# The order of GpSimd's work around the seam between attention and experts, in a spiking-attention and mixture-of-experts kernel

## The reference

```
Q, K, V = spike(layer_norm(xn @ W.T + b) * gain + beta - 1)        # values 0 or 1, 16 heads of 16
out     = einsum((16 - hamming(Q, K) + log_position_bias) * scale, V)
s       = spike(layer_norm(spike(out - 0.5) @ Wo.T + bo) * go + betao - 1)

xr      = rms_norm(xn);  ids = nearest of 8 centroids, for each row
h       = xr @ up_w[ids]  (256 -> 1024);  a, g = halves of h
y       = (a * silu(g)) @ down_w[ids]     (512 -> 256)
result  = x + s * silu(y + xn)
```

## Time and profile before

| | us |
|---|---|
| median of 3 runs | 425.05 |
| lowest and highest | 421.77, 425.44 |
| profiled execution, its own time | 424.03 |
| its span, first to last instruction | 422.2 |
| mean granted TensorE clock in it | 0.962 of full |

### The profile page before, as it was taken

The page is one execution under the profiler, slowest core; times in us unless marked ns, Lnnn a source line. Parts: engine busy times, 40 slices in busy tenths (PEclk is TensorE's granted clock), DMA queues, the critical chain, the costliest instruction groups (busy, mean ns, idle before and its releaser), DMA issues.

```text
span 422.2 us, 10208 instructions
## 1 busy us (share of the span) xinstructions
PE 380.5 (90%) x2652; PEld 319.7 (76%) x2662; DVE 326.6 (77%) x821; ACT 237.5 (56%) x614; POOL 246.7 (58%) x338
## 2 busy tenths in 40 slices
PE   5596999999997697999499999999999999999992
PEld 5475878778875586888378888888888888888881
DVE  5965888888867989886557767778777787878883
ACT  1555877878875053463445555555555565555551
POOL 1444777778865044456827656665666666666542
PEclk9888999999998898999879999999999999999997
DMA  6448456866630020231651222222222223221100
GB/s 198 167 148 276 147 154 178 259 225 186 184 117 2 0 77 26 76 104 49 183 191 46 84 80 63 69 78 91 87 70 75 84 81 103 92 89 57 37 15 0
DMA packets 31649, 44.86 MB, mean 106 GB/s; under 512 B 4041, under 2 KB 25714, under 8 KB 31492
## 3 DMA queue, kind: packets, MB, share of 16 engines
q1 hardware_dynamic: 25040, 29.38, 22.6%
q0 software_dynamic: 6240, 14.71, 11.7%
q10 hardware_dynamic: 340, 0.42, 0.3%
HBM read 36.28 MB, written 15.61 MB: 123 GB/s over the span
## 4 chain that ended last, share of the span: by engine, by line
PE 60%; DMA 10%; DVE 10%; POOL 7%; issue 7%; ACT 3%; POOLq 1%; SPq 1%; DVEq 0%; ACTq 0%
PE bank L558 22%; PE bank L576 12%; DMA xs<-in_x 6%; PE bank L400 6%; PE bank L446 4%; PE bank L540 4%; DMA row_a<-rows_a,slot_id 3%; PE bank L478 3%; PE bank L529 2%; POOL inv_std L1142 2%; PE bank L450 2%; POOL sq L1167 2%; PE bank L458 1%; DVE up_lo L1039 1%; POOL rs L1161 1%
## 5 line engine op out<-in xcount | busy, mean ns | idle before, releaser
L1079 DVE TENSOR_TENSOR d_lo<-down_sb,d_hi 128x1024 fp32r<-128x1024 f32 x39 | 47.8, 1226 | 33.2 <-ACT d_hi L739 33.2
L1204 POOL DMA_INDIRECT row_a<-rows_a,slot_id x39 | 40.1, 1029 | 46.8 <-DVE e_o L1093 44.9
L739 ACT ACTIVATE d_hi<-down_sb 128x1024 fp32r x39 | 41.3, 1060 | 45.3 <-PE bank L576 33.2
L1248 POOL DMA_INDIRECT out_x<-e_o,slot_id x39 | 44.6, 1142 | 20.6 <-issue 14.4
L558 PE MATMUL bank<-up_hi,e_xh 128*128 x156 | 52.5, 418 | 0.0
L1210 POOL DMA_INDIRECT row_s<-rows_s,slot_id x39 | 41.0, 1050 | 15.7 <-issue 11.6
L558 PE MATMUL bank<-up_lo,e_xh 128*128 x156 | 48.7, 393 | 0.0
L558 PE MATMUL bank<-up_hi,e_xl 128*128 x156 | 48.4, 391 | 0.0
L400 PE MATMUL bank<-w_hi,x_hi 128*128 128x264 f32 (+1 forms) x128 | 42.3, 412 | 0.8 <-DVE dots L888 0.8
L664 ACT ACTIVATE junk<-bank 128x256 bf16<-128x256 f32 x96 | 36.0, 379 | 9.1 <-PE bank L404 8.2
L687 ACT ACTIVATE junk<-bank 128x256 bf16<-128x256 f32 x32 | 12.0, 379 | 50.1 <-PE bank L480 50.1
(11 more groups left out here) (210 smaller groups left out, 1036.6 us busy)
## 6 DMA issues: line engine op xcount, KB each, us to landing
up_raw<-in_up_w SPq DMA_DIRECT2D x16, 512.0 KB, 5.1
rows_a<-xn SPq DMA_DIRECT2D x32, 128.5 KB, 2.5
xs<-in_x SPq DMA_DIRECT2D x8, 512.0 KB, 3.4
rows_a<-in_x SPq DMA_DIRECT2D x8, 512.0 KB, 5.5
down_sb<-in_down_w SPq DMA_DIRECT2D x8, 512.0 KB, 4.5
rows_s<-s_out SPq DMA_DIRECT2D x8, 256.0 KB, 2.4
blk_tab<-in_blocks SPq DMA_DIRECT2D x1, 1024.0 KB, 5.6
row_a<-rows_a,slot_id POOLq DMA_INDIRECT x39, 3.4
```

What stands on the lines that cost most here:

```text
L739: act.activation(d_hi[:, :, :], down_sb[:, bass.ds(e, 1), :, :].rearrange("p a c n -> p (a c) n"), ACT.Copy).then_inc(d_high, 1)
L1079: V.tensor_tensor(d_lo[:, :, :], down_sb[:, bass.ds(e, 1), :, :].rearrange("p a c n -> p (a c) n"), d_hi[:, :, :].bitcast(F32), ALU.subtra ...
L1204: G.indirect_dma_start(row_a[s % 4][:, :], None, rows_a, bass.IndirectOffsetOnAxis(ap=slot_id[:, s:s + 1], axis=0), bounds_check=N - 1, oo ...
L1248: G.indirect_dma_start(out, bass.IndirectOffsetOnAxis(ap=slot_id[:, s:s + 1], axis=0), e_o[s % 4][:, :], None, bounds_check=N - 1, oob_is_ ...
```

## The change

On POOL, in the attention loop. `norms_out` of the chunk comes first in every chunk. The clearing of the row buffers, with its waits, moves from chunk 5, ahead of the norms, to chunk 4, behind the norms and ahead of the low part of expert 6. The first four `gather_a` stood directly behind the clearing; now tiles 0 and 1 are gathered in chunk 5 behind the norms, and tiles 2 and 3 in chunk 6 behind the norms. The low part of expert 7 moves from between the norms of chunks 6 and 7 to behind the norms of chunk 7. In chunks 0 to 3 the order is the same. No other engine's code changes.

```diff
--- before.py
+++ after.py
@@ -1220,7 +1220,8 @@
             for e in range(2):
                 low_part_up(e)
             for c in range(NCH):
-                if c == 5:
+                norms_out(c % 2, c // 2)
+                if c == 4:
                     pool.wait_ge(slots_made, 1)
                     for k in range(4):
                         G.memset(row_a[k][:, :], 0.0)
@@ -1230,13 +1231,12 @@
                         pool.wait_ge(row_put[k], 16 * NT // 4)
                     pool.wait_ge(x_copied, 16 * NT // 4)
                     pool.wait_ge(rows_clear, 1)
-                    for k in range(4):
-                        gather_a(k)
-                norms_out(c % 2, c // 2)
                 if c < NCH - 3:
                     low_part_up(c + 2)
-                if c == NCH - 2:
-                    low_part_up(E - 1)
+                if c in (5, 6):
+                    for k in range(2):
+                        gather_a(2 * (c - 5) + k)
+            low_part_up(E - 1)
             for k in range(2):
                 pool.wait_ge(s_put[k], 16 * NCH // 2)
             for k in range(4):
```

## The result

| | us |
|---|---|
| changed kernel, median of 20 runs | 421.62 (417.88 to 423.35) |
| kernel before, median of 20 runs beside them | 425.46 (421.30 to 428.19) |
| ratio | 0.990, 95% interval 0.9878 to 0.9923 |
| changed kernel once more on another chip (below) | ratio 0.9904, interval 0.9872 to 0.9936 |
| profiled execution, its span | 419.71, 417.9 |

The change saves 3.84 us by the medians, and 3.3 to 5.2 by the interval. The prediction was 419.8 in 417.0 to 423.0, so the direction and the range held; the saving is 1.4 us smaller than the 5.2 between the forecast and the median that it started from.

The account below looks back on a forecast made before the run. POOL's order, clearing and gathers ahead of norms 5, was taken to hold PE at the seam. Profiled 424.03 - 4.8 = 419.2 and median 425.05 - 4.8 = 420.3 gave a forecast of 419.8 us, range 417.0 to 423.0.

Parts of the forecast that it names:

- The bound and the cause: Between attention and experts, PE idles 5.71 us for a_sp of chunk 7; POOL's order costs PE some 6 us, once.
- ACT next, then the loads: At the experts' start: ACT's unmoved e_xh holds PE until 208.1, then down-weight loads landing at 212.4 hold tile 0's silu.
- The size: At e_h of expert tile 0: 213.2 instead of 218.02, 4.8 us less, with unchanged work from there.
- faster by over 1%: Whole kernel: time falls by more than 4.25 us; chance 0.57, against 0.38 within 1% and 0.05 slower.
- I take 0: Chunk 4: the moved clearing slows DVE's low parts by 0 more; up to 1.2 us was left for the upper end.
- The low part of expert 7 "nothing": POOL: moving this 2.47 us piece behind norms 7, to about 211.3, costs nothing, as it ends before s_out has landed.
- The first gather: POOL, chunk 5: starts at 199.7, lands at 203.3, or 205.2 if slowed; lateness up to 1.5 us hides.
- a first gather after 205.6: Sign at the seam: the forecast would be wrong if the first gather landed later than 205.6.
- Rival 2: Experts' start: loads land at 213.7 and PE's clock falls; 1.9 us less, 422.7, or 421.2 with only one; chance 0.27.
- rival 1: Experts' start: loads land by 211.3 and DVE's order decides; e_h at 212.1, 5.9 us less, 418.5; chance 0.14.
- Rival 4: Experts' stage: reuse of four row buffers costs 1.4 us per two tiles; 434 at ten such rounds; chance 0.04.

Follow-up runs that it names:

- the last experiment: Changed kernel plus ACT's load wait behind the first silu and expert 7's ACT and DVE parts moved later, gathers two by two; ratio to the kernel before 1.0000.
- norms-first kernel: Kernel before with only the norms of chunk 5 moved ahead of the clearing and all four gathers; ratio to the kernel before 1.0011.

## Why the prediction was right, and where it was off

- **The bound and the cause** held: PE's wait was POOL's order, by way of s_out of chunk 5 and a_sp of chunk 7. The wait is gone with the order, and early loads alone move nothing.
- **ACT next, then the loads** held, to a tenth: e_xh at 208.1 was forecast, 208.36 - 0.67 (the anchor's difference) = 207.69 came. The silu was forecast at 212.5, and 213.47 - 0.67 = 212.8 came. The sum of the DMA bytes at 320 GB/s, with the gathers counted in, is what gave this: from 202 to 213.4 they moved at 310 GB/s on average, and the longest load took 9.8 us to land. The Trainium skill (DMA: Bandwidth & Descriptors, Queues, rings and completion order) has each DMA engine go round-robin between the queues. By that the loads pay for the gathers, and the trace agrees (9.8 us instead of 7.3); gathers pay for loads too (6.2 us instead of 3.6), which I had only as 1 us on the first gather's upper end.
- **The size**: e_h 4.8 us earlier was forecast; 4.5 and, in the second execution, 4.8 came. The medians show 3.84, and the ratio on the second chip 4.1 (0.96% of 427). The term that was mis-sized is small: 0.3 us at e_h, as the last load landed 0.3 later than summed. Another 0.8 of the 1.8 us between 419.8 and 421.62 is the start: the profile that the sum went out from lay 1.4 us under the median of 20 runs, and the forecast added only 0.6. The remaining 0.7 is inside the interval. Of the three outcomes, "faster by over 1%" had 0.57, and the result lies on its border: 3.84 us are 0.9% by the medians, the ratio is 0.990, and its interval reaches to both sides. So the range and the mechanism are what held; that greater chance is neither borne out nor refuted.
- **The clearing**: "I take 0" held, and more. DVE's two low parts take 2.47 us beside the clearing, not 4.57; it was POOL's own low part that had held them, and not both as the prediction reasoned. The rule of the Trainium skill (GPSIMD Engine Reference, Key points) that GpSimd contends with VectorE instructions of two SBUF inputs agrees with 1.27 against 2.91 us in the last experiment, where POOL reads two tensors, and not with the clearing, which reads none.
- **The low part of expert 7 "nothing"** was wrong by the trace: its move brings e_h 0.8 to 1.1 us forward. In time it is 1.1 us by the midpoints, which the intervals do not tell from nothing. The step looked only at what lies behind the piece in its new place, and not at what it holds up in its old one once norms 7 have become urgent.
- **The first gather** was put at 205.2 at worst, with 1.5 us to spare. It landed in time (PE turned at 204.31) because it was issued 2.1 us before the loads. Issued 3.6 us later, in the norms-first kernel, it was there 6.6 us later, and that and, by the waits, the late norms 6 took the whole gain. The prediction named "a first gather after 205.6" as what would make it wrong, but not how near that was.
- **Rival 2** came half true: the clock did fall, in the first expert tile of one execution, but under the cover of the loads. With the loads out of the way e_h gained only 5.0 us on the kernel before (13.80 - 8.82) and not rival 1's 5.9, since PE at the half clock stood there. Rival 4, the reuse of the row buffers, did not appear: from 228 to 300 the gather stands on the chain once, at 244.93, where it did three times, and on the whole chain of the experts two and three times in the two executions, against three. The chains of the other kernels show one to five such places without a pattern, so that is not shown to be the change's doing.

## What to carry to other kernels

An in-order engine that serves two masters, here norms for the running stage and set-up for the next, should do the piece that somebody waits for first, and each piece then counts by its place and not by its length. Ask also what the early release sets free elsewhere: here SP's 2 MB of loads came 6 us earlier, made a gather twice as slow where it was issued behind them, and became the next bound. Two gathers at a time or four made no difference that the time shows with the other engines' orders as in the change, and over 1% with the new ones, so test it again when these move.

## What the runs showed of the hardware that was not expected

- A gather of 128 rows of 2 KB lands in 3.6 to 3.7 us alone, in 4.1 to 5.1 with a lead of 2.1 us on 2 MB of loads (seven executions), in 5.9 and 6.2 with a lead of 1.2 us, and in 7.35, by PE's turn, when issued 1.5 us behind them.
- Clearing a buffer on GpSimd does not slow VectorE's two-input instructions beside it (2.47 us for two); a two-input GpSimd instruction that began first holds one for most of the time that it has still to run (2.91 us instead of 1.27, with 1.8 left).
- In four executions PE's granted clock went from the 2.4 to the 1.2 GHz level in the first expert tile, behind a wait of only 1.73 to 1.88 us. The length of the wait alone does not decide it: behind waits of 2.32, 2.84 and 2.94 us in other kernels PE went on at 1.00, and behind 2.53 and 2.57 it did not. What does decide it, these runs do not show.
